# A fused cross-attention and expert layer: the first score visit, the expert tables and the last tiles are put in another order

## The chip, the core and the metric

The kernel runs on one core of a Trainium2 chip. The core has five engines that run side by side and wait for each other through semaphores: TensorE (PE in the rows; PEld is its weight load), VectorE (DVE), ScalarE (ACT), GpSimd (POOL) and SyncE (SP), which here issues most of the DMA transfers. Each engine works through its own list of instructions in the order in which they are written. The metric is the device time of one execution in microseconds (us).

## What is computed

For 16 batches of 256 tokens with 256 features, an attention layer over a context, then a layer of which one half is shared and the other half is one of two experts per token:

```python
x = x + xattn(layernorm(x), ctx, ctx, Wq, Wk, Wv, Wo)
x = x + ffn(layernorm(x), gate_w, w1, b1, w2, b2, sw1, sb1, sw2, sb2)
# xattn: 16 heads of 16; each block of 64 keys has a softmax of its own; sum over the blocks of a band
# ffn, n tokens, D = 256, hidden 1024:
top1 = argmax(softmax(x @ gate_w.T))
masked = x[None] * one_hot(top1).T[:, :, None]            # zero rows for the expert not chosen
h = relu(einsum("end,edh->enh", masked, w1) + b1)
routed = (einsum("enh,ehd->end", h, w2) + b2).sum(0)
shared = relu(x @ sw1 + sb1) @ sw2 + sb2
return routed + shared
```

## The kernel before

One iteration does one batch (i) of attention, the shared half of the batch before (n = i - 1) and one tile of 256 routed tokens (m = i - 2). The tokens are queued in DRAM by expert; a tile is 256 rows of one expert's queue. Iterations 0 to 3 are written out (iteration 0 has no shared half, 0 to 2 have no tile), 4 to 14 are a hardware loop, 15 is written out, and behind it come the rest of tile 14, the shared half of batch 15, tile 15 and two left tiles (`FIRST_LEFT`, `SECOND_LEFT`), one for each expert's remainder.

All operands of products are split in a high half (ScalarE) and a low half (VectorE or GpSimd), and products are three matmuls.

- **Scores.** `visit(i, v)` (v = 0 to 3) makes four banks of scores (L528), two in `work`, two in `nd`; VectorE takes the negative maximum of each bank (`maximum`, L1081). A bank can be written again when its maximum is taken. `maxima` (L541) transposes all of them, and ScalarE, VectorE and two DMAs (`shift`) write them as extra rows of `QP`. `scores_t` (L551) makes the transposed scores, ScalarE the exponentials, `values` (L567) the products, VectorE a reciprocal and a product for each of eight pairs (`divide`, L1088 and L1090). Q and K come back from DRAM in two halves (`spread`); visit 0 uses half 0.
- **The end of an iteration.** `attention_out` (L581), `project_out` (L595), residual (`x`, L1096), norm, with the reciprocal deviation from GpSimd (L1312, L1315), `norm2_apply` (`xhat`, L1054), `prep_tokens` (L483), the halves of `Xs` (L1034), then the shared half's first up. `norm1_apply` is the same form on `xin`, for the batch after the next.
- **Units.** A hidden layer of 1024 is four units. `up` (L477, 12 matmuls) makes a unit in `hid`, ScalarE its two halves (`relu`, L884), GpSimd the low half (`hl`, L1321), `down` (L639, 12 matmuls) adds it to `acc`. A tile's first down is preceded by two matmuls of a `level` row.
- **Tables.** What the expert not chosen gives for a zero row is a constant: `table(e)` (L691, 24 matmuls) for each expert, from `table_relu` (ScalarE) and `table_low` (GpSimd), through `level_sum` and `level_low` (L1169). Before, table 0 runs in iteration 1 in front of `attention_out`, table 1 behind the first visit of iteration 2, and `shared_down(1, 0)` waits for both level rows.
- **Tiles.** `ranks` and `place` (GpSimd, L1344 to L1378) find each token's row in its queue; `queue_x` and `queue_y` scatter the tokens; SP waits for them, then loads W1 of the tile's expert and the tile's tokens `xt` (L324); `tile_tokens` (L483, from `xt`) transposes them. Behind iteration 15, `left` gives the rows of the remainders, SP writes padding rows behind both queues (`xq<-T`, `yq<-T`), loads the first expert's W1 again, and then the two left tiles.

## Time and profile before

| | before |
|---|---|
| median of three runs | 997.09 us (995.03 to 997.75) |
| the profiled execution | 994.35 us, span 992.2 us, mean granted TensorE clock 0.932 |
| TensorE busy | 830.1 us, 84% of the span |
| VectorE, ScalarE, GpSimd busy | 64%, 45%, 44% |
| loop iteration, from one `attention_out` to the next | 52.4 to 53.9 us |
| from the first up of tile 14 to the last matmul | 80.6 us |

The span goes from the first to the last instruction that the profiler recorded; the execution is 2 us longer. A time in front of a row is its start, from the span's start. In brackets stands how long the engine had been idle before the row and what it waited for. A granted clock of 1.00 is TensorE's full clock.

### The profile page before, as it was taken

Reading aid. Unit: us, or ns where it says so; the run is one execution under the profiler, and the core shown is the slowest. Engines: PE = TensorE matmul, PEld = TensorE weight load, DVE = VectorE, ACT = ScalarE, POOL = GpSimd, SP = SyncE. Lnnn points to the kernel's source line nnn. Section 1 sums busy time; section 2 is a strip of 40 time slices with the busy share of each in tenths; the row PEclk is TensorE's granted clock in tenths of the full one; section 3 lists DMA queues with packets and bytes.
Section 4 is the critical chain, followed back from the end, with each engine's and each line's share of the span. In section 5 each row is a group of like instructions: output and inputs, shape, how many; then the busy total and the mean of one; then the engine's idle time right before and its main releaser. Section 6 shows DMA issues by size and latency. Waiting matters only on the chain.

```text
span 992.2 us, 22821 instructions
## 1 busy us (share of the span) xinstructions
PE 830.1 (84%) x7862; PEld 682.5 (69%) x7862; DVE 631.1 (64%) x1126; ACT 446.9 (45%) x980; POOL 440.8 (44%) x816
## 2 busy tenths in 40 slices
PE   3277868789898989899998989898989899887874
PEld 2246647477786868686868777786868686757874
DVE  3665585666868586867677776868586867663000
ACT  2353342436354545445454636354545445453432
POOL 3653322324344453626353534444453635253734
PEclk9586888979999999999999999999999999998988
DMA  8666230343535262525343443535262534222720
GB/s 258 164 161 223 75 97 6 107 154 115 163 94 195 74 205 81 159 86 157 101 154 127 133 153 116 170 91 195 74 198 88 159 100 136 96 69 100 245 65 22
DMA packets 97386, 128.17 MB, mean 129 GB/s; under 512 B 14655, under 2 KB 82623, under 8 KB 97088
## 3 DMA queue, kind: packets, MB, share of 16 engines
q1 hardware_dynamic: 89760, 107.89, 35.1%
q0 software_dynamic: 6624, 18.95, 5.7%
q10 hardware_dynamic: 960, 0.79, 0.5%
q8 instruction: 25, 0.41, 0.2%
q14 instruction: 17, 0.14, 0.0%
HBM read 90.80 MB, written 37.04 MB: 129 GB/s over the span
## 4 chain that ended last, share of the span: by engine, by line
issue 33%; POOL 24%; PE 20%; DVE 10%; DMA 7%; ACT 2%; POOLq 1%; SPq 1%; ACTq 1%; DVEq 0%
POOL hl L1321 11%; PE hid L477 5%; PE acc L639 4%; PE nd L567 4%; DVE T L1088 4%; DVE nmax L1081 3%; POOL out L1401 2%; POOL xq L1384 2%; PE work L551 2%; DMA QP<-scratch_m 2%; POOL c_lo_t L1306 1%; POOL rstd L1315 1%; POOL idle L1302 1%; DMA scratch_m<-mT 1%; POOL yq L1391 1%
## 5 line engine op out<-in xcount | busy, mean ns | idle before, releaser
L1321 POOL TENSOR_TENSOR hl<-h,hh 128x256 fp32r<-128x256 f32 x264 | 192.2, 735 | 361.5 <-ACT hh L884 359.8
L1088 DVE RECIPROCAL T<-nd 128x256 f32<-128x256 f32 x128 | 224.3, 1753 | 87.1 <-PE nd L567 78.5
L874 ACT ACTIVATE PT<-work 128x512 f32<-128x512 f32 x256 | 140.2, 606 | 90.6 <-PE work L551 90.6
L884 ACT ACTIVATE h<-hid,bias 128x256 f32<-128x256 f32 x144 | 68.5, 476 | 157.1 <-PE hid L477 155.6
L477 PE MATMUL hid<-Xs,W 128*128 128x256 f32 x816 | 122.6, 305 | 8.7 <-DVE Xs L1034 8.7
L477 PEld LDWEIGHTS hid<-Xs,W 128*128 128x128 f32 x816 | 110.8, 207 | 15.3 <-issue 9.1
L639 PE MATMUL acc<-w_hi,hh 128*128 128x256 f32 (+1 forms) x528 | 113.3, 297 | 3.5 <-DVE level L1169 3.5
L477 PE MATMUL hid<-Xr,W 128*128 128x256 f32 x768 | 105.1, 286 | 2.1 <-DVE Xr L1034 2.1
L639 PE MATMUL acc<-w_lo,hh 128*128 128x256 f32 (+1 forms) x528 | 106.2, 283 | 0.0
L477 PEld LDWEIGHTS hid<-Xr,W 128*128 128x128 f32 x768 | 94.8, 189 | 14.9 <-issue 10.7
L1081 DVE TENSOR_REDUCE nmax<-work 128x8 f32<-128x512 f32 x128 | 82.2, 685 | 33.4 <-PE work L528 33.1
L567 PE MATMUL nd<-PT,V 128*32 128x256 f32 x1024 | 84.5, 402 | 12.5 <-DVE T L1090 9.4
L639 PEld LDWEIGHTS acc<-w_hi,hh 128*128 128x128 f32 x528 | 82.3, 193 | 16.4 <-issue 10.6
L884 ACT ACTIVATE h<-hid,bsel 128x256 f32<-128x256 f32 x120 | 57.7, 481 | 71.4 <-PE hid L477 68.4
L639 PE MATMUL acc<-w_hi,hl 128*128 128x256 f32 (+1 forms) x528 | 85.3, 284 | 1.5 <-POOL hl L1321 1.5
L639 PEld LDWEIGHTS acc<-w_lo,hh 128*128 128x128 f32 x528 | 82.6, 193 | 0.0
L1081 DVE TENSOR_REDUCE nmax<-nd 128x8 f32<-128x512 f32 x128 | 82.0, 683 | 0.0
L567 PE MATMUL nd<-PT,bsum 128*32 128x256 f32 x1024 | 81.1, 388 | 0.0
L551 PE MATMUL work<-QP,KP 56*128 56x256 f32 x512 | 66.2, 337 | 16.6 <-DMA QP<-scratch_m 14.2
L551 PEld LDWEIGHTS work<-QP,KP 56*128 56x128 f32 x512 | 39.6, 190 | 50.5 <-ACT PT L874 22.0
L639 PEld LDWEIGHTS acc<-w_hi,hl 128*128 128x128 f32 x528 | 72.5, 193 | 2.6 <-POOL hl L1321 2.6
L884 ACT ACTIVATE hh<-hid,bias 128x256 fp32r<-128x256 f32 x144 | 68.5, 476 | 0.0
(178 smaller groups left out, 1384.0 us busy)
## 6 DMA issues: line engine op xcount, KB each, us to landing
W<-w1q SPq DMA_DIRECT2D x64, 512.0 KB, 6.1
KP<-scratch_k SPq DMA_DIRECT2D x192, 64.0 KB, 2.3
QP<-scratch_q SPq DMA_DIRECT2D x180, 64.0 KB, 2.3
scratch_k<-T SPq DMA_DIRECT2D x16, 512.0 KB, 3.5
scratch_q<-T SPq DMA_DIRECT2D x16, 512.0 KB, 3.3
yt<-yq SPq DMA_DIRECT2D x17, 260.0 KB, 2.9
xt<-xq SPq DMA_DIRECT2D x17, 256.0 KB, 3.7
xin<-x SPq DMA_DIRECT2D x16, 256.0 KB, 3.5
```

The lines of the kernel that those rows point to most:

```text
L477: mm = nc.tensor.matmul(dst, R(s), R(m), start=n == 0, stop=n == len(steps) - 1)
L551: mm = nc.tensor.matmul(banks[s][:, SEQ * t:SEQ * t + SEQ], R(KP[rows, p, P * t:P * t + P]), R(QP[rows, p, :]), start=True, stop=True)
L567: mm = nc.tensor.matmul(nd[r:r + 32, p % 2, kind, :], V[:, t, 2 * p + s, :] if kind == 0 else bsum[:, :], PT[:, (2 * p + s) % 4, t, :], st ...
L639: mm = nc.tensor.matmul(acc[:, t, :], R(h[:, u % 2, a, P * t:P * t + P]), R(row), start=first, stop=u == UNITS - 1 and h is hl and a == 1, ...
L874: nc.scalar.activation(PT[:, j % 4].rearrange("p t q -> p (t q)"), work[:, BANK[("st", j)], :], ACT.Exp).then_inc(sem["exp_done"], 1)
L884: last = nc.scalar.activation(dst, hid[:, u % 2, a, :], ACT.Relu, bias=bias[:, 2 * u + a:2 * u + a + 1])
L1081: nc.vector.tensor_reduce(nmax[:, t, :].rearrange("q (b s p) -> q s p b", s=2, b=NBLK) [:, s, 2 * g:2 * g + 2, :], bank.rearrange("q (n b ...
L1088: nc.vector.reciprocal(T[:, p, :], nd[:, p % 2, 1, :]).then_inc(sem["inverted"], 1)
L1302: nc.gpsimd.tensor_tensor(idle[:, site:site + 1], eps[0:1, 0:1], eps[0:1, 0:1], ALU.add)
L1321: nc.gpsimd.tensor_tensor(R(hl[:, u % 2, a]), h32[:, u % 2, a], hh[:, u % 2, a], ALU.subtract).then_inc(sem["hl_done"], 1)
L1384: pool.indirect_dma_start(out=xq, out_offset=bass.IndirectOffsetOnAxis(ap=pos[:, t:t + 1], axis=0), in_=xhat2[:, t, :], in_offset=None).th ...
L1401: pool.indirect_dma_start(out=out_rows, out_offset=bass.IndirectOffsetOnAxis(ap=rows, axis=0), in_=yt[:, t, 0:D], in_offset=None, **partly) \
```

## The change

TensorE's, VectorE's, ScalarE's and GpSimd's lists are reordered; no product is added or left out.

- `visit(i + 1, 0)` stands behind `attention_out(i)`; its four maxima stand two ahead of the residual and two ahead of `norm2_apply`. `norm1_apply` moves to VectorE's end of the iteration. The bank of `wo` changes, and with it what each bank waits for.
- An iteration begins with visit 1, then both ups, the ranks, the first down. In iterations 1 and 2 `shared_down` 1 stands ahead of visit 3, not behind it.
- Table 0 stays in iteration 1, table 1 goes to the same place in iteration 2; each level row is finished an iteration later, kept in `yt` in place of `xt`; the shared downs wait for `level_sum` of their own table only.
- In iteration 15 `tile_up` 1 stands ahead of the first `scores_t`, `tile_tokens` ahead of a down, `tile_down` 0 of the next tile ahead of `prep_tokens`; GpSimd takes the reciprocal deviation ahead of the low halves, and waits for the shift rows ahead of `place`.
- From unit 2 of tile 14 on, the low halves are VectorE's (`last_low`), `tile_tokens` stands ahead of the tile before's unit 3, and SP loads the first left tile's tokens ahead of its wait for `y_queued`. GpSimd leaves out its small operation `apart(7)` where the tile is not the loop's.

```diff
                 load_w1(W1[:, 0], 0, u, "w1_again")
+            sp.wait_ge(sem["padded"], 64)
+            rows = [sp.value_load(left[0:1, e:e + 1], min_val=0, max_val=QROWS - TILE) for e in range(2)]
+            sp.wait_ge(sem["xr_full"], FIRST_LEFT - 1)
+            load_tile_x(FIRST_LEFT, rows[0])
             sp.wait_ge(sem["y_queued"], 32 * BATCH)
             load_tile_y(last, row)
-            sp.wait_ge(sem["padded"], 64)
-            rows = [sp.value_load(left[0:1, e:e + 1], min_val=0, max_val=QROWS - TILE) for e in range(2)]
-            for m, row in zip((FIRST_LEFT, SECOND_LEFT), rows):
-                sp.wait_ge(sem["xr_full"], m - 1)
-                load_tile_x(m, row)
+            sp.wait_ge(sem["xr_full"], SECOND_LEFT - 1)
+            load_tile_x(SECOND_LEFT, rows[1])
...
                         pe.wait_ge(sem["r_done"], n - 2)
-                    elif n == 2:
-                        pe.wait_ge(sem["y_done"], 2)
-                    elif n == 1:
-                        pe.wait_ge(sem["level_made"], 2)
+                    elif n > 0:
+                        pe.wait_ge(sem["level_sum"], n)
...
                 n, m = i - 1, i - 2
-                visit(i, 0)
-                if type(i) is int and i == 2:
-                    table(1)
+                visit(i, 1, more)
                 if shared:
                     shared_up(n, 0)
+                    shared_up(n, 1)
                     ranks(n, claim(i, ("rk", 0), tile=tile))
-                    shared_up(n, 1)
-                visit(i, 1)
-                if shared:
                     shared_down(n, 0)
-                visit(i, 2)
+                visit(i, 2, more)
                 if shared:
                     shared_up(n, 2)
-                if tile:
                     shared_down(n, 1)
-                visit(i, 3)
+                visit(i, 3, more)
                 if tile:
                     shared_up(n, 3)
                     shared_down(n, 2)
-                elif shared:
-                    shared_down(n, 1)
                 maxima(i)
...
                 for p in range(PAIRS):
-                    fill(n, m, tile, p, expert)
+                    if more or p != 0:
+                        fill(n, m, tile, p, expert)
                     if p + 1 < PAIRS:
...
                     values(i, p)
                 if tile:
                     tile_up(m, 3)
-                if type(i) is int and i == 1:
-                    table(0)
+                elif shared:
+                    table(i - 1)
                 attention_out(i, more)
+                if more:
+                    visit(i + 1, 0)
+                else:
+                    tile_tokens(m + 1, work[:, BANK["v", 0], :])
                 if tile:
                     tile_down(m, 2, expert)
-                if not more:
-                    tile_tokens(m + 1, work[:, BANK["v", 0], :])
                 project_out(i, more)
...
             pe.wait_ge(*low_done(2 * STAGES - 1))
             pe.wait_ge(*low_done(len(pieces) - 1))
@@ -788,15 +808,13 @@
             iteration(3, True, True, True)
             with pe.Fori(4, BATCH - 1) as i:
                 iteration(i, True, True, True)
-            iteration(BATCH - 1, True, True, False)
+            expert = iteration(BATCH - 1, True, True, False)
 
             last = BATCH - 1
+            tile_up(last - 1, 2)
+            tile_down(last - 1, 1, expert)
             pe.wait_ge(sem["x2_lo"], BATCH)
             ranks(last, work[:, 2, :])
-            expert = pe.value_load(chosen[0:1, 1:2], min_val=0, max_val=1)
-            tile_down(last - 1, 0, expert)
-            tile_up(last - 1, 2)
-            tile_down(last - 1, 1, expert)
             tile_up(last - 1, 3)
             tile_down(last - 1, 2, expert)
             shared_up(last, 0)
...
                 tile_down(m, 0, expert)
                 tile_up(m, 2, weights, tokens)
                 tile_down(m, 1, expert)
-                tile_up(m, 3, weights, tokens)
                 if after:
                     tile_tokens(after[0], work[:, (after[0] - last) % 2, :])
+                tile_up(m, 3, weights, tokens)
                 tile_down(m, 2, expert)
...
 
+            def last_low(g, u):
+                for a in range(2):
+                    dve.wait_ge(sem["relu_done"], 2 * g + a + 1)
+                    nc.vector.tensor_tensor(R(hl[:, u % 2, a]), h32[:, u % 2, a], hh[:, u % 2, a],
+                                            ALU.subtract).then_inc(sem["last_low"], 1)
+
             def level_sum(e):
-                dve.wait_ge(sem["table_full"], 2)
-                nc.vector.tensor_tensor(xt[:, e, :], acc[:, e, :], bias2[:, :], ALU.add) \
+                dve.wait_ge(sem["table_full"], e + 1)
+                nc.vector.tensor_tensor(yt[:, e, 0:D], acc[:, e, :], bias2[:, :], ALU.add) \
                     .then_inc(sem["level_sum"], 1)
...
                 norm1 = more and (type(i) is not int or i + 2 < BATCH)
-                for v in range(VISITS):
+                for v in range(1, VISITS):
                     for j in range(4 * v, 4 * v + 4):
                         maximum(i, j)
                     splits(i, v + 1)
-                    if type(i) is int and i == 2 and v == 0:
-                        level_sum(0)
-                        level_sum(1)
-                    if shared and v == 0:
+                    if shared and v == 1:
                         rank_tokens(n)
-                    if type(i) is int and i == 2 and v == 0:
-                        level_low(0)
-                        level_low(1)
+                    if type(i) is int and i in (2, 3) and v == 1:
+                        level_low(i - 2)
...
                 low(i, "at_hi", work_bank("at"), a_hi[:, :, :], a_lo[:, :, :], "at_lo")
                 splits(i, 10)
-                if norm1:
-                    norm1_apply(i + 2)
-                if not more:
+                if more:
+                    maximum(i + 1, 0)
+                    maximum(i + 1, 1)
+                else:
                     tile_low(m + 1, work_bank("v"))
                 residual(i)
                 norm2_stats(i)
+                if more:
+                    maximum(i + 1, 2)
+                    maximum(i + 1, 3)
+                else:
+                    finish_tile(m)
                 norm2_apply(i)
...
-                if tile:
+                if tile and more:
                     finish_tile(m)
+                if shared and not tile:
+                    level_sum(n)
+                if norm1:
+                    norm1_apply(i + 2)
 
...
             nc.vector.memset(pad[:, :, D:YCOLS].bitcast(I32), SKIPPED).then_inc(sem["pad_made"], 1)
+            last_low(tile_unit(last - 1, 2), 2)
+            last_low(tile_unit(last - 1, 3), 3)
+            last_low(shared_unit(last, 0), 0)
             finish_tile(last - 1)
+            last_low(shared_unit(last, 1), 1)
+            last_low(shared_unit(last, 2), 2)
             tile_low(last, work[:, 0, :].rearrange("p (c t) -> p c t", c=2))
+            last_low(shared_unit(last, 3), 3)
+            last_low(tile_unit(last, 0), 0)
             finish_shared(last)
             for m, tokens in ((last, Xs), (FIRST_LEFT, Xr), (SECOND_LEFT, None)):
+                last_low(tile_unit(m, 1), 1)
+                last_low(tile_unit(m, 2), 2)
                 if tokens is not None:
                     tile_low(m + 1, work[:, (m + 1 - last) % 2, :].rearrange("p (c t) -> p c t", c=2), tokens)
+                last_low(tile_unit(m, 3), 3)
+                if tokens is not None:
+                    last_low(tile_unit(m + 1, 0), 0)
                 finish_tile(m)
...
                 if shared:
+                    if not more:
+                        pool.wait_ge(sem["shift_spread"], 32 * (i + 1))
                     place(n, choosing=type(i) is not int or i > 1)
                     queue_x(n)
...
                     tile_hidden(m, 3)
-                if type(i) is int and i == 1:
-                    table_low(0)
+                if shared and not tile:
+                    table_low(n)
                 if norm1:
                     reciprocal_deviation(i + 2, 0)
+                reciprocal_deviation(i, 1)
                 if not more:
                     tile_hidden(m + 1, 0)
-                reciprocal_deviation(i, 1)
 
...
 
             last = BATCH - 1
+            tile_hidden(last - 1, 1)
             send_out(last - 2)
-            tile_hidden(last - 1, 1)
-            tile_hidden(last - 1, 2)
             place(last, at=2)
-            tile_hidden(last - 1, 3)
             queue_x(last)
-            shared_hidden(last, 0)
             nc.gpsimd.tensor_copy(left[:, 0:1], next0[:, :])
             nc.gpsimd.tensor_copy(left[:, 1:2], next1[:, :])
             nc.gpsimd.tensor_scalar(left[:, 2:3], count[:, :], -1.0, float(BATCH * SEQ + QUEUE), ALU.mult, ALU.add)
             nc.gpsimd.tensor_copy(left[:, 3:4], count[:, :]).then_inc(sem["left_made"], 1)
-            shared_hidden(last, 1)
             send_out(last - 1)
-            shared_hidden(last, 2)
-            shared_hidden(last, 3)
-            tile_hidden(last, 0)
             queue_y(last)
-            for u in range(1, UNITS):
-                tile_hidden(last, u)
-            for m in (last, FIRST_LEFT):
-                tile_hidden(m + 1, 0)
+            for m in (last, FIRST_LEFT, SECOND_LEFT):
                 send_out(m)
```

ScalarE's list changes with these (its halves follow the units), and the claims of banks and the semaphores' names.

TensorE, behind the last division of iteration 3, before and after (L581, in the changed kernel L596, is `attention_out`; L639, now L657, are the first matmuls of `tile_down` 2):

```order
L581 MATMUL work<-T,hsum 32x2x64 x16
L639 ISA
L639 MATMUL acc<-w_hi,hh 128x256 x2
L639 REGISTER_ALU
L639 MATMUL acc<-w_lo,hh 128x256 x2
```

```order
L596 MATMUL work<-T,hsum 32x2x64 x16
L541 MATMUL work<-KP,QP 128x256 x4
L541 MATMUL nd<-KP,QP 128x256 x4
L657 ISA
L657 MATMUL acc<-w_hi,hh 128x256 x2
```

The score visit (`work` and `nd` from `KP`, `QP`) is put between them.

TensorE, from `prep_tokens` of iteration 3 into the loop's first iteration, before (the score visit, L528, is visit 0) and after (L541, it is visit 1; L488 is the up, L627 to L631 are the ranks):

```order
L483 MATMUL work<-id,xhat 128x128 x4
L789 UNCONDITIONAL_BRANCH
L469 REGISTER_ALU
L522 ISA
L528 MATMUL work<-KP,QP 128x256 x4
L520 REGISTER_ALU
L528 MATMUL nd<-KP,QP 128x256 x4
L621 ISA
L477 MATMUL hid<-Xs,W 128x256 x12
L612 MATMUL work<-mask,before 128x2
L614 MATMUL work<-mask,ones 128x2
L616 MATMUL work<-mask,ones 128x1
```

```order
L480 REGISTER_ALU
L535 ISA
L541 MATMUL work<-KP,QP 128x256 x4
L531 ISA
L541 MATMUL nd<-KP,QP 128x256 x4
L636 ISA
L488 MATMUL hid<-Xs,W 128x256 x12
L636 REGISTER_ALU
L488 MATMUL hid<-Xs,W 128x256 x12
L627 MATMUL work<-mask,before 128x2
L629 MATMUL work<-mask,ones 128x2
L631 MATMUL work<-mask,ones 128x1
```

The ranks stood between the two ups, and the next visit behind the second; now the two ups and the ranks follow each other, and the first down comes next.

SP behind iteration 15, from the second set of W1 loads, before and after:

```order
L320 DMA W<-w1q 128x1024 x4
L330 ISA
L330 DMA yt<-yq 128x2x260
L443 TENSOR_LOAD left
L443 ISA x2
L443 TENSOR_LOAD left
L443 ISA x2
L324 ISA
L324 DMA xt<-xq 128x2x256
```

```order
L328 DMA W<-w1q 128x1024 x4
L451 TENSOR_LOAD left
L451 ISA x2
L451 TENSOR_LOAD left
L451 ISA x2
L332 ISA
L332 DMA xt<-xq 128x2x256
L338 ISA
L338 DMA yt<-yq 128x2x260
```

The load of `xt` for the first left tile and the reading of `left` moved ahead of the load of `yt`.

## Rows read from the trace of the kernel before

**Rows 1.** TensorE's waits in iterations 4 to 14: total us, times, longest
```profile
PE work L483 <- DVE xhat L1054: 11.5, 11, 1.1
```
**Rows 2.** TensorE in order of time, iteration 6: start, us, line, tile, what it waited for
```profile
374.82 0.50 PE L528 MATMUL work<-KP,QP 48*128 48x256 f32 x4
...
375.97 0.50 PE L639 MATMUL acc<-w_hi,hh 128*128 128x256 f32 x2
...
377.57 0.50 PE L528 MATMUL work<-KP,QP 48*128 48x256 f32 x4
...
378.55 1.68 PE L477 MATMUL hid<-Xs,W 128*128 128x256 f32 x12
...
381.52 0.50 PE L528 MATMUL work<-KP,QP 48*128 48x256 f32 x4
...
382.19 1.68 PE L477 MATMUL hid<-Xs,W 128*128 128x256 f32 x12
```
**Rows 3.** TensorE in iteration 7, and the granted clock over its 4 us
```profile
424.03 2.93 PE L477 MATMUL hid<-Xs,W 128*128 128x256 f32 x12 [0.58 <-DVE Xs L1034]
...
424.00:428.00 4.00, 3.97 (x23) 3.88 (x24) 3.96 (x13) 0.87 (x3) 0.00 (x0) 0.62 0.30 117
```
**Rows 4.** VectorE at iteration 6's end, in order of time
```profile
418.09 0.69 DVE L1096 TENSOR_TENSOR x<-work,x 128x512 f32<-128x512 f32 x1 [1.00 <-PE work L595]
...
421.01 0.73 DVE L1054 TENSOR_SCALAR xhat<-x,mv,rstd 128x256 f32<-128x256 f32 x2 [1.16 <-POOL rstd L1315]
```
**Rows 5.** SP in order of time, iteration 6: half 0 of Q
```profile
402.38 2.78 SPq L259 DMA_DIRECT2D QP<-scratch_q  x6
```
**Rows 6.** TensorE in iterations 1 and 2, in order of time
```profile
136.84 1.08 PE L581 MATMUL work<-T,hsum 128*32 128x128 f32 x32 [0.15 <-DVE T L1090]
...
144.25 1.09 PE L483 MATMUL work<-id,xhat 128*128 128x128 f32 x4 [2.44 <-DVE xhat L1054]
...
160.90 0.80 PE L639 MATMUL acc<-w_hi,hh 128*128 128x256 f32 x2 [3.47 <-DVE level L1169]
...
200.10 1.94 PE L581 MATMUL work<-T,hsum 128*32 128x128 f32 x32 [3.27 <-DVE T L1090]
...
209.61 0.63 PE L483 MATMUL work<-id,xhat 128*128 128x128 f32 x4 [1.31 <-DVE xhat L1054]
```
**Rows 7.** TensorE in iteration 15, in order of time
```profile
869.55 0.50 PE L551 MATMUL work<-QP,KP 56*128 56x256 f32 x4 [2.73 <-DMA QP<-scratch_m]
```
**Rows 8.** Behind iteration 15: busy times, TensorE's waits, two ups of one pair apart
```profile
898.40:979.10 80.70, 65.27 (x510) 62.89 (x508) 10.04 (x32) 33.47 (x84) 46.53 (x81) 0.92 0.34 109
...
PE work L483 <- DMA xt<-xq: 5.7, 1, 5.7
PE work L483 <- DVE xhat L1054: 3.0, 1, 3.0
...
PE hid L477 <- DVE Xr L1034: 2.1, 2, 1.1
...
958.43 1.58 PE L477 MATMUL hid<-Xs,W 128*128 128x256 f32 x12
...
961.28 1.56 PE L477 MATMUL hid<-Xs,W 128*128 128x256 f32 x12
```
**Rows 9.** Behind iteration 15: GpSimd's `place`, SP's loads; issues with us to landing
```profile
915.60 0.20 POOL L1344 TENSOR_TENSOR own<-ids,rank 128x2 f32<-128x2 f32 x1
...
925.43 0.37 SPq L324 DMA_DIRECT2D xt<-xq  x1
...
933.29 0.37 SPq L435 DMA_DIRECT2D yq<-T  x1
...
946.39 0.39 SPq L324 DMA_DIRECT2D xt<-xq  x1
...
yq<-T SPq DMA_DIRECT2D x2, 260.0 KB, 7.0
xt<-xq SPq DMA_DIRECT2D x2, 256.0 KB, 2.7
```

106 lines of the change are left out of this document (63 added, 43 removed).

## The prediction, made before the changed kernel was run

> **What bounds the kernel now.** I read the page first (it has TensorE busy for 84% of the span), then TensorE's waits over eleven loop iterations, one iteration of TensorE and VectorE in order of time, then the places where an iteration is not like the others: iterations 1 and 2, iteration 15, and the stretch behind it. In the loop TensorE is nearly full. What it waits for in eleven iterations is 11.5 us for `xhat` (1.05 each) [rows 1], beside 1.5 us each for the divisions and less for other things. The outer stretches are poorer: in iteration 2 it waits 3.47 us for `level` and 3.27 us for `T` [rows 6], before the scores of iteration 15 it waits 2.73 us [rows 7], and behind iteration 15 it is busy for 65.27 of 80.70 us [rows 8]. A second loss is the clock: one first-layer unit takes 1.68 us at full clock [rows 2] and 2.93 us in iteration 7, where the granted clock over 4 us was 0.62, a stretch partly at 1.2 GHz, after TensorE had idled before `xhat` and `Xs` [rows 3]. By their starts, five of iterations 4 to 15 have such a slow first unit, at some 1.25 us each.
>
> **Part 1, the loop: the first visit moves to the end of the iteration before.** A visit whose banks are free takes 382.19 - 381.52 = 0.67 us. The second took 375.97 - 374.82 = 1.15, the third 378.55 - 377.57 = 0.98 [rows 2]: 0.48 and 0.31 us of waiting for VectorE, which at an iteration's start has sixteen maxima to take, as fast as it can. Now it has twelve there; the other four go into holes of the end: VectorE idles 1.00 us before the residual and 1.16 us before `xhat` [rows 4], and a pair of maxima takes 1.28 us there (a page row: 685 ns each). Added at the start is `norm1_apply`, 0.73 us by the same form in [rows 4], against 2.5 us that went. So both waits should go: 0.79 us, and some 0.6 us in an iteration with a slow first unit, which gives VectorE time. The visit itself costs 0.67 us at either place: it is ahead of `project_out` now, so `wo_full`, the residual and `xhat` come 0.67 us later, while visit 1 stands where visit 0 stood between `xhat`'s transposes and the first unit; the 1.05 us wait for `xhat` stays. The second pair of maxima fills the hole before `xhat` with 0.1 us to spare or less: I charge 0.05. New is that the first down follows the second up at once. Its low halves on GpSimd come about 2.6 us after the first up's end and are wanted about 2.6 us after it, so I charge 0.05 and keep 0.6 as the other end. Sum: 0.6 us for each of iterations 3 to 15, 13 x 0.6 = **7.8 us**; ends 0 and 10. Slow first units I leave as many as they are, since the idle time ahead of them keeps its shape; ends: none (-6) and one in every iteration (+9).
>
> **Part 2, the tables over two iterations.** Before, both tables and the level rows lie on iteration 2's path. `xhat`'s transposes of the last batch start at 144.25 and the first down at 160.90, 16.65 us [rows 6]. In the new order only these stand between: from transposes to first unit 2.55 us (the chain through ScalarE and VectorE in iteration 1's start, visit 1 beside it) and two ups partly at the low clock, 5.0 us; that is 7.55, so 9.1 us go. Iteration 1 itself I put 0.8 us earlier: its first residual no longer stands behind `norm1_apply`, which waited for GpSimd, and its visits lose their waits. From the first down to the transposed maxima nothing changes: before 8.6 us, now a down, a visit, an up and a down (5.4 us) and the 3.17 us from visit 3's begin to its last maximum, which no down covers any more. The new 1.07 us of `level` low halves on VectorE hide beside an up and a down. 9.1 + 0.8 = 9.9 us; 9.8 with 0.1 for a late maximum. The second table now runs in iteration 2 ahead of `attention_out`, where TensorE waits 3.27 us for `T`. In iteration 1 the first table ran in that place, and what was left of the wait was 0.15 us [rows 6]: it is free. It also keeps the clock: from `T` to `xhat` iteration 1 took 144.25 - 136.84 = 7.41 us and iteration 2, where `attention_out` ran 1.94 us instead of 1.08, took 9.51 [rows 6]; 2.1 us between them, of which I take 1.5 (the visit and the maxima may take 0.1, and the end may be slow for the reason of Part 1). Sum 9.8 + 1.5 = **11.3 us**; ends 9 and 13.
>
> **Part 3, iteration 15.** With `tile_up` 1 ahead of the first `scores_t`, it fills 1.6 of the 2.73 us that TensorE waits for the shift rows [rows 7], and the first values follow at once. Before, it ran behind that wait. VectorE's divisions start by that much earlier and set the rest of the iteration: **1.7 us**; ends 0 and 2.2.
>
> **Part 4, behind iteration 15.** From its first `tile_up` (898.47) to the last matmul 80.6 us pass. Work: 20 ups and 20 downs. A pair takes 961.28 - 958.43 = 2.85 us [rows 8], less with the level matmuls taken out, 2.83: 56.6 us; four level sets at 0.25, four transposes at 0.36 and the ends make 59.4. What the change does to the rest: the `xhat` wait of 3.0 us [rows 8] and the waits for the mask and for `yt` behind it go, since GpSimd takes the reciprocal deviation before the low halves and `tile_down` 0 stands in front of the transposes; the two waits for `Xr` (1 us each) go, as an up and a down now stand between transposes and use; the low halves of VectorE take away the waits for GpSimd, 1.5 us of the 15.4 that TensorE idles here (80.70 - 65.27) (nothing if they are late too). The largest wait, 5.7 us for `xt` [rows 8], does not go whole. Count from the first `tile_up` as zero. `ranks` stand at 7.7, `place` can start at 8.1 (before 17.1, [rows 9]), and since the load of `xt` came 925.43 - 915.60 = 9.8 us after that start with one pair of low halves between, now gone, it is issued at 16.6. Landing took 2.7 us [rows 9]: 19.3, wanted at 19.1, so 0.5 us is lost. The next load of `xt` waits for the padding: the last pad was issued 933.29 - 925.43 = 7.9 us after the first load and takes 7.0 us to land [rows 9], so 31.5; reading the two rows cost 1.35 us, and landing 2.7: **35.6**. TensorE is there at 31.9. It waits 3.7 us, not 5.7, but 15 us sooner (before, that load landed at 50.6), and restarts as slowly as before. From there 29.9 us are left as before (up 3 added, one `Xr` wait and 0.4 us of the last low halves off). End at 65.5 against 80.6: **15.0 us**; ends 12 and 19.5 (the load lands in time and the clock stays). The trace shows no load of `xt` issued while the second set of W1 loads is in flight; its nearest rows are 2.7 us on an empty queue and 7.0 us for a pad behind loads [rows 9]. I take 2.7, since by 33 most of that set has landed.
> On this the Trainium skill's page DMA: Bandwidth & Descriptors, "Issuing engines are not separate DMA queues", says that all DMAs run on the same 16 engines and interleave. The 7.0 us of a pad agrees, and by the rule alone the load would land some 1 us later and the sum be 1 us smaller. The page SBUF — State Buffer, "Who interferes with whom", says that a two-input operation of VectorE contends with GpSimd's reads; no row used here shows it in this stretch, and by it the 1.5 us of the low halves could come back in part.
> The final `send_out` loses one small operation of GpSimd: 0.3 us.
>
> **Sum.** 7.8 + 11.3 + 1.7 + 15.0 + 0.3 = 36.1 us. The profiled execution took 994.35 us (span 992.2), which gives 958.3; the median of the timed runs is 2.7 us above it, so 997.1 - 36.1 = **961.0 us**.
>
> **Rivals.**
> A, the load in time: pads and W1 loads land sooner and `xt` costs nothing, 4.5 us more gained: 956.5. For it: the wait is a difference of two long chains. Against: the pads' 7.0 us.
> B, the low clock in each iteration: seven more slow first units at 1.25 us: 961.0 + 8.8 = 969.8. For it: `xhat` is 0.05 us later and the idle time stays. Against: the added visit in front of it is work.
> C, the wait of `nmax` is replaced by one for GpSimd's low halves, since nothing stands between second up and first down: 0.6 us in 13 iterations: 968.8. For it: wanted and ready fall together. Against: GpSimd has nothing else to do there, its 0.73 us are short of a down's 1.5.
> D, the tables or iteration 15 give half or less, because the second table's low half is late and `T`'s hole doesn't hold it (5.5 us for 24 matmuls at the low clock against 3.27): 967 to 971.
> E, **slower than before**: VectorE takes two maxima ahead of the residual, so that a late visit holds up `wo`'s chain and with it all of the iteration's end. The visit needs the spread Q and K of the next batch, and each us that they come late is paid in each of 12 iterations. The kernel is slower from 36.1 / 12 = 3.0 us of lateness on; at 3.5 us it takes 1003. The last of half 0 is issued by 405.2 in one iteration [rows 5] and lands some 2.4 us later, the visit would come at 415: 7 us of room, so the spread would have to take 10 us longer than it does.
> F, the change doesn't do what it says: the waits go but every stage is held by VectorE at another place: within 0.3% of before. VectorE is busy 64% of the span; I see no such place.
>
> **Chances.** Forecast (957 to 965) 0.50, A 0.18, B 0.11, C 0.09, D 0.08, F 0.02, E 0.02. The range holds the forecast, A, C, B and most of D: 953 to 971. Faster by over 0.3% (3 us, about what a measurement can tell from no change) 0.96, within 0.3% 0.02, slower 0.02.
>
> **What the profile after would show.** Part 1: visits of 0.67 us everywhere in the loop, periods near 51.7 and 53.1 us instead of 52.4 and 53.7, no `nmax` wait; a wait of `acc` for `hl` would be C; a first unit of 2.9 us in each iteration B. Part 2: no table between `xhat` and the first unit, first down 7.5 us behind the transposes, no `T` wait in iteration 2. Part 3: two `scores_t` in a row, first values 1.7 us sooner. Part 4: one wait of some 4 us for `xt` some 32 us behind the first `tile_up`, none for `Xr` and `xhat`; 65 us in all. The prediction is wrong if TensorE shows a wait in each iteration that is not among these.

## The result

| | before | changed, first measurement | changed, second measurement |
|---|---|---|---|
| median of the runs | 996.06 us (4 runs, 992.78 to 997.75) | 954.64 us (4 runs, 952.14 to 957.01) | 953.58 us (6 runs, 948.65 to 956.68) |
| ratio to before | | 0.9588 (0.9546 to 0.9629) | 0.9574 (0.9539 to 0.9609) |
| profiled execution, span | 994.35, 992.2 us | 952.14, 950.3 us | 952.34, 950.5 us |

The second measurement's ratio is to its own runs of the kernel before (996.53 us, 11 runs). The kernel is 41.4 us faster in the first measurement (forecast 36.1, 961.0 us, range 953 to 971). By stretches of the two kernels' traces, the second trace of the changed kernel behind the slash:

| stretch | before | changed | gained | forecast |
|---|---|---|---|---|
| start to `attention_out` of iteration 3 | 255.3 | 241.0 / 239.3 | 14.3 / 16.1 | 11.9 |
| eleven periods, to that of iteration 14 | 583.3 | 571.6 / 571.7 | 11.7 / 11.6 | 6.6 |
| one period, to that of iteration 15 | 54.1 | 52.7 / 52.6 | 1.5 / 1.6 | 2.3 |
| from there to the last matmul | 86.3 | 71.9 / 73.8 | 14.4 / 12.5 | 15.0 |
| behind the last matmul | 13.2 | 13.2 / 13.2 | 0.0 | 0.3 |

The forecast column is the prediction's parts put into these stretches: Part 2 and one 0.6, eleven times 0.6, Part 3 and one 0.6, Part 4, the end. "Period" is the time from one `attention_out` to the next.

### The profile page after: what moved, and what is told of

Its sections match the earlier page's. It is cut to its first block, busy times and chain, and to the rows that moved or that the text cites. A ratio compares the mean times of both kernels' runs of the same rounds, so it can differ in the third digit from the quotient of the medians.

```text
span 950.3 us, 22814 instructions
## 1 busy us (share of the span) xinstructions
PE 812.9 (86%) x7862; PEld 673.6 (71%) x7862; DVE 645.9 (68%) x1162; ACT 445.9 (47%) x980; POOL 416.1 (44%) x773
## 4 chain that ended last, share of the span: by engine, by line
PE 59%; DVE 17%; DMA 11%; ACT 4%; issue 3%; SPq 2%; POOL 1%; ACTq 1%; POOLq 0%; DVEq 0%
PE hid L488 17%; PE acc L657 14%; PE nd L582 11%; DVE T L1104 7%; PE work L566 5%; DMA QP<-scratch_m 5%; DMA scratch_m<-mT 3%; DVE nmax L1097 3%; PE work L610 3%; PE work L541 2%; PE work L596 2%; PE work L494 1%; DVE xhat L1070 1%; DVE T L1106 1%; ACT h L902 1%
## 5 line engine op out<-in xcount | busy, mean ns | idle before, releaser
L1364 POOL TENSOR_TENSOR hl<-h,hh 128x256 fp32r<-128x256 f32 x228 | 166.7, 737 | 309.5 <-ACT hh L902 309.1
L488 PE MATMUL hid<-Xs,W 128*128 128x256 f32 x816 | 118.3, 301 | 8.2 <-DVE Xs L1050 8.2
L488 PEld LDWEIGHTS hid<-Xs,W 128*128 128x128 f32 x816 | 108.5, 205 | 15.2 <-issue 8.8
L657 PE MATMUL acc<-w_hi,hh 128*128 128x256 f32 (+1 forms) x528 | 111.2, 292 | 0.0
L657 PE MATMUL acc<-w_lo,hh 128*128 128x256 f32 (+1 forms) x528 | 104.8, 280 | 0.0
L488 PE MATMUL hid<-Xr,W 128*128 128x256 f32 x768 | 104.1, 285 | 0.0
L488 PEld LDWEIGHTS hid<-Xr,W 128*128 128x128 f32 x768 | 94.0, 188 | 12.3 <-issue 10.7
L582 PE MATMUL nd<-PT,V 128*32 128x256 f32 x1024 | 84.5, 402 | 11.7 <-DVE T L1106 8.4
L657 PEld LDWEIGHTS acc<-w_hi,hh 128*128 128x128 f32 x528 | 80.7, 189 | 8.9 <-issue 7.2
L657 PE MATMUL acc<-w_hi,hl 128*128 128x256 f32 (+1 forms) x528 | 84.3, 282 | 0.1
L657 PEld LDWEIGHTS acc<-w_lo,hh 128*128 128x128 f32 x528 | 81.1, 190 | 0.0
L657 PEld LDWEIGHTS acc<-w_hi,hl 128*128 128x128 f32 x528 | 71.6, 189 | 0.8 <-POOL hl L1364 0.3
```

Of the source, the lines that this page charges most:

```text
L488: mm = nc.tensor.matmul(dst, R(s), R(m), start=n == 0, stop=n == len(steps) - 1)
L582: mm = nc.tensor.matmul(nd[r:r + 32, p % 2, kind, :], V[:, t, 2 * p + s, :] if kind == 0 else bsum[:, :], PT[:, (2 * p + s) % 4, t, :], st ...
L657: mm = nc.tensor.matmul(acc[:, t, :], R(h[:, u % 2, a, P * t:P * t + P]), R(row), start=first, stop=u == UNITS - 1 and h is hl and a == 1, ...
L1364: nc.gpsimd.tensor_tensor(R(hl[:, u % 2, a]), h32[:, u % 2, a], hh[:, u % 2, a], ALU.subtract).then_inc(sem["hl_done"], 1)
```

## The profile after

**The loop.** TensorE in order of time in iterations 6 and 7 (start, us, line, operation, tiles, shape, number of instructions, and in brackets the idle time ahead and what ended it). L596 is `attention_out`, L541 a visit, L488 an up, L494 the transposes:

```profile
344.22 1.08 PE L596 MATMUL work<-T,hsum 128*32 128x128 f32 x32 [1.53 <-DVE T L1106]
345.23 0.51 PE L541 MATMUL work<-KP,QP 48*128 48x256 f32 x4
...
345.90 0.50 PE L657 MATMUL acc<-w_hi,hh 128*128 x2
...
354.96 3.09 PE L488 MATMUL hid<-Xs,W 128*128 128x256 f32 x24 [0.56 <-DVE Xs L1050]
...
359.72 0.50 PE L541 MATMUL work<-KP,QP 48*128 48x256 f32 x4
...
360.38 1.68 PE L488 MATMUL hid<-Xs,W 128*128 128x256 f32 x12
...
395.72 1.08 PE L596 MATMUL work<-T,hsum 128*32 128x128 f32 x32 [1.53 <-DVE T L1106]
```

Every visit now takes 0.67 us (345.90 - 345.23, 360.38 - 359.72 = 0.66), where [rows 2] has 1.15 and 0.98. Both first ups follow each other (3.09 for 24 matmuls), and a period is 51.50 us where nothing disturbs it. The waits for `xhat` and `Xs` stay as they were in [rows 1] and [rows 3]. TensorE's waits from the `attention_out` of iteration 3 to that of iteration 15 have no `nmax` and no `hl`; the two longest (total us, times, longest) are these:

```profile
PE work L596 <- DVE T L1106: 18.5, 12, 1.6
PE work L494 <- DVE xhat L1070: 12.5, 12, 1.1
```

**VectorE** at the same place of iteration 7, which answers to [rows 4]. The first pair of maxima ends 1.13 us ahead of the residual, the second ends as `xhat` can start, and the `xhat1` step (L1070 again, at 407.83) stands last:

```profile
398.11 1.28 DVE L1097 TENSOR_REDUCE nmax<-work 128x8 f32<-128x512 f32 x2
400.52 0.69 DVE L1112 TENSOR_TENSOR x<-work,x 128x512 f32<-128x512 f32 x1 [1.12 <-PE work L610]
...
402.19 1.26 DVE L1097 TENSOR_REDUCE nmax<-nd 128x8 f32<-128x512 f32 x2
403.44 0.73 DVE L1070 TENSOR_SCALAR xhat<-x,mv,rstd 128x256 f32<-128x256 f32 x2
```

**The clock.** Two of the eleven periods are longer, 53.00 and 54.36 us. The second is of a kind that the kernel before does not show. Stretches of TensorE behind the `attention_out` at 655.11 (window, its length, busy time of TensorE, of its weight loads, of VectorE, ScalarE and GpSimd, granted clock, DMA share, GB/s):

```profile
657.00:659.00 2.00, 2.00 (x10) 2.00 (x11) 1.77 (x3) 0.00 (x0) 0.08 (x1) 0.50 0.71 247
...
667.00:671.00 4.00, 3.59 (x18) 3.60 (x19) 3.96 (x13) 0.51 (x3) 0.00 (x0) 0.57 0.00 0
```

TensorE had idled 1.53 us before `attention_out`. Behind that and the visit the clock is at 0.50, which is 1.2 GHz, the third down takes 2.92 us, and the first ups at 667.4 are slow again: 2.8 us for the iteration. Below, a period with one or both of these is called disturbed.

Iteration 15 is not free of it in either trace of the changed kernel. In the first the clock falls behind the wait for the shift rows, in the second in the first ups:

```profile
846.00:848.00 2.00, 2.00 (x22) 0.94 (x20) 1.41 (x1) 0.79 (x2) 1.73 (x9) 0.51 0.03 8
```
```profile
822.00:824.00 2.00, 2.00 (x12) 2.00 (x11) 2.00 (x7) 0.00 (x0) 0.00 (x0) 0.53 0.06 19
```

In the traces of experiments 7 and 10, which leave iteration 15 as it is, it stays at full clock, and the period takes 51.23 and 50.97 us, not 52.66 and 52.55.

**Iterations 1 and 2**, TensorE, answering to [rows 6]. L709 is a table; some rows between are left out:

```profile
133.13 1.08 PE L596 MATMUL work<-T,hsum 128*32 128x128 f32 x32
...
141.21 0.91 PE L494 MATMUL work<-id,xhat 128*128 128x128 f32 x4 [2.45 <-DVE xhat L1070]
...
148.66 0.48 PE L657 MATMUL acc<-w_hi,hh 128*128 128x256 f32 x2
...
183.78 0.58 PE L709 MATMUL acc<-w_hi,hh 128*128 128x256 f32 x1
...
187.65 1.08 PE L596 MATMUL work<-T,hsum 128*32 128x128 f32 x32
...
195.73 0.82 PE L494 MATMUL work<-id,xhat 128*128 128x128 f32 x4 [2.46 <-DVE xhat L1070]
```

From the transposes to the first down 7.45 us pass (forecast 7.5, before 16.65), the second table fills the hole before `T`, and from `T` to `xhat` it is 8.08 us (forecast 9.51 - 1.5 = 8.0).

**Behind iteration 15**, which answers to [rows 8] and [rows 9]. TensorE's waits (the first up of tile 14 starts at 871.04), GpSimd's `place` and the last queued row, and SyncE's issues:

```profile
893.41 0.66 PE L494 MATMUL work<-id,xt 128*128 128x128 f32 x4 [2.52 <-DMA xt<-xq]
...
899.03 0.62 PE L657 MATMUL acc<-w_hi,hl 128*128 128x256 f32 x4
...
902.09 0.50 PE L697 MATMUL acc<-level,level_row 128*128 x2 [1.03 <-DVE yp L1163]
...
908.48 0.66 PE L494 MATMUL work<-id,xt 128*128 128x128 f32 x4 [1.64 <-DMA xt<-xq]
```
```profile
879.77 0.19 POOL L1387 TENSOR_TENSOR own<-ids,rank 128x2 f32<-128x2 f32 x1 [0.38 <-DVE count L1149]
...
882.66 0.50 POOL L1410 TENSOR_SCALAR chosen<-ahead,which,next 128x1 int32<-128x1 f32 x1
...
886.08 0.97 POOL L1427 DMA_INDIRECT xq<-xhat,pos  x1 [0.30 <-issue]
```
```profile
885.62 0.34 SPq L328 DMA_DIRECT2D W<-w1q  x1
890.01 0.37 SPq L332 DMA_DIRECT2D xt<-xq  x1
890.56 1.39 SPq L328 DMA_DIRECT2D W<-w1q  x3
892.15 0.33 SPq L359 DMA_DIRECT2D bsel<-b  x1
...
897.04 2.02 SPq L328 DMA_DIRECT2D W<-w1q  x4
903.88 0.39 SPq L332 DMA_DIRECT2D xt<-xq  x1
```

The last matmul ends at 937.13: 66.1 us, 68.1 in the second trace (forecast 65.5, before 80.6). The same columns as above over the whole stretch, first and second trace, for which [rows 8] has 80.70 us, 65.27 busy and 0.92:

```profile
871.04:937.14 66.10, 60.77 (x509) 59.41 (x507) 25.25 (x66) 33.69 (x84) 21.54 (x41) 1.00 0.40 132
```
```profile
869.20:937.31 68.11, 62.25 (x509) 61.02 (x507) 25.92 (x66) 33.62 (x84) 21.43 (x41) 0.97 0.40 129
```

So TensorE idles 5.3 and 5.9 us and not 15.4; the other 4.4 and 3.0 us are the same matmuls in less busy time, at a mean clock of 1.00 and 0.97 and not 0.92. There are two waits for `xt`, at +19.9 and +35.8 us, and a new one of 1.03 us for `yp`. Why `yp` is late stands in ScalarE's and VectorE's rows:

```profile
899.24 0.47 ACT L902 ACTIVATE h<-hid,bsel 128x256 f32<-128x256 f32 x1 [2.15 <-DMA bsel<-b]
```
```profile
900.85 0.43 DVE L1180 TENSOR_TENSOR hl<-h,hh 128x256 fp32r<-128x256 f32 x1 [0.31 <-ACT hh L902]
901.19 0.68 DVE L1162 TENSOR_TENSOR yp<-acc,x 128x512 f32<-128x512 f32 x1
```

`bsel`, the bias of the chosen expert, is issued behind four loads of W1 and lands 7.1 us later, the relu of the last tile's first unit waits 2.15 us for it, VectorE's low halves wait for the relu, and `yp` is queued behind them, though the shared expert's last matmuls had ended by 899.03 + 0.62 = 899.65.

## Experiments

All start from the changed kernel. Times are medians of five or six runs.

**1. The changed kernel once more.**

> The changed kernel once more, for a second trace of it beside the others. If the number of iterations in which TensorE's clock is low at the end or in the first unit is a matter of chance (2 of 12 in its first trace, and 2, 2 and 7 in the three kernels that keep its loop), it may be anything from 0 to 7 here, every undisturbed period is 51.5 to 51.7 us again, and the time is 952 to 960, moving with that number by 1.4 to 2.9 us each. If the number belongs to the kernel, it is 2 and the time 952 to 956.

953.58 us. The undisturbed period is 51.45 to 51.72 again; two of eleven periods are disturbed, one of each kind (52.8 and 54.4). The number came out the same, but with the traces below it is no property of the kernel: it was 2 to 6 in the kernels that keep its loop.

**2. The visit back to the iteration's start.** Its four maxima go back there with it, and `norm1_apply` stands ahead of the residual again.

```diff
-                visit(i, 1, more)
+                visit(i, 0)
                 if shared:
                     shared_up(n, 0)
-                    shared_up(n, 1)
                     ranks(n, claim(i, ("rk", 0), tile=tile))
+                    shared_up(n, 1)
+                visit(i, 1)
...
-                    visit(i + 1, 0)
```

> The changed kernel with Part 1 alone undone: visit 0 stands at the iteration's start again, with its four maxima there and the xhat1 step in front of the residual; the first two shared ups have ranks and visit 1 between them. Theory (Part 1 as forecast): the visits' waits of some 0.48 and 0.31 us come back in each iteration, the undisturbed period goes from 51.55 back to 52.4 us, and 12 to 13 iterations give 8 to 11 us; with about as many slow first units as in the changed kernel (2 of 12) 963 to 966 us. Rival 1: the visit's place also decides how often TensorE's clock falls ahead of the first unit: then 4 or more of the 12 iterations show a first unit of 2.9 us, and the time is 967 to 970. Rival 2: the loop's gain comes from elsewhere, the period stays under 51.9 and the time under 958.

973.17 us (971.03 to 975.24), beyond both expectations. An undisturbed period, L591 being `attention_out`, is 455.58 - 403.23 = 52.35 us, and the waits for `nmax` are back:

```profile
403.23 1.08 PE L591 MATMUL work<-T,hsum 128*32 128x128 f32 x32 [1.54 <-DVE T L1100]
...
455.58 1.08 PE L591 MATMUL work<-T,hsum 128*32 128x128 f32 x32 [1.54 <-DVE T L1100]
```
```profile
PE nd L538 <- DVE nmax L1091: 3.2, 11, 0.3
```

The span is 969.5, 19.1 more than the mean of the changed kernel's two: 3.5 to iteration 3 (1.8 in the period from iteration 0 to 1, 2.2 in the next), 12.2 in eleven periods, 2.3 in iteration 15 and 1.1 behind it. Of the 12.2, 11 x 0.87 = 9.6 are the undisturbed period (52.47 us in the mean against 51.60), and 2.6 that six periods are disturbed and not two. Iteration 15 and the stretch behind it also have more low clock here. So the visit is worth some 13 us beside the clock, the first two iterations being the uncertain part (see Part 1 below). Of the waits' list only 0.3 us an iteration is named `nmax`; the period shows the rest, so this list alone would have undersized the part.

**3. The tables back in iteration 2**, with both level rows ahead of its first shared down.

```diff
                 visit(i, 1, more)
+                if type(i) is int and i == 2:
+                    table(1)
...
-                elif shared:
-                    table(i - 1)
+                elif i == 1:
+                    table(0)
                 attention_out(i, more)
```

> The changed kernel with Part 2 alone undone: both tables are made for iteration 2's first shared down, the second one at that iteration's start. Theory (Part 2 as forecast): from the transposes of xhat to iteration 2's first down it takes some 16 us and not 7.45, TensorE waits for T again by 3.3 us in iteration 2 and from T to xhat takes 9.5 us and not 8.1: 11 us slower than the changed kernel (9 to 13), 964 to 968. Rival: of the 14.3 us by which the changed kernel is ahead at iteration 3, 3 and more came from earlier stretches and the visit; then the tables give back 8 us or less, 960 to 962.5.

965.22 us. TensorE waits for `level` ahead of the first down and for `T`:

```profile
140.59 0.63 PE L494 MATMUL work<-id,xhat 128*128 128x128 f32 x4 [2.45 <-DVE xhat L1080]
...
156.25 0.79 PE L657 MATMUL acc<-w_hi,hh 128*128 128x256 f32 x2 [4.12 <-DVE level L1201]
...
195.40 1.93 PE L596 MATMUL work<-T,hsum 128*32 128x128 f32 x32 [3.27 <-DVE T L1116]
```

That is 15.66 us from transposes to first down against 7.45, and from `T` to `xhat` 10.17 against 8.08. At iteration 3's `attention_out` (249.6) it is 9.5 us behind the mean of the changed kernel's two traces. The median says 10.6 to 11.6; the loop is the changed kernel's, but this trace had six disturbed periods (15.7 us), so the trace's stretch is the better measure: 9.5. That is below the expected 11 and in its range of 9 to 13.

**4. Iteration 15's second `tile_up` back behind the scores.**

```diff
                     tile_up(m, 0)
-                    if not more:
-                        tile_up(m, 1)
```

> The changed kernel with Part 3 alone undone: in iteration 15 the second tile_up stands behind the first scores_t again. Theory (Part 3): TensorE waits some 2.7 us and not 1.5 for the shift rows, attention_out of iteration 15 comes 1.2 to 1.7 us later, and the time is 956 to 956.5. Rival: VectorE's divisions make up for it by attention_out; nothing changes, 954.6 within 0.3.

960.52 us (957.28 to 967.02); the median does not settle 2 us, since the runs are 10 us apart. The trace says more. From the transposed maxima to `attention_out` it takes 870.87 - 838.79 = 32.08 us, and 865.28 - 835.15 = 30.13 in the changed kernel. The wait for the shift rows is 2.98 us and 1.52, and behind the longer one the displaced `tile_up` itself runs 2.93 us:

```profile
838.79 0.27 PE L556 MATMUL work<-id,nmax 128*128 128x128 f32 x1
...
846.48 0.79 PE L566 MATMUL work<-QP,KP 56*128 56x256 f32 x4 [2.98 <-DMA QP<-scratch_m]
847.20 2.93 PE L488 MATMUL hid<-Xr,W 128*128 128x256 f32 x12
...
870.87 1.08 PE L596 MATMUL work<-T,hsum 128*32 128x128 f32 x32 [1.61 <-DVE T L1101]
```

The 1.95 us between the two are not all the order's, for the clock is low in both places. From the first `scores_t` behind the wait to the third `tile_up` it takes 12.28 us here and 10.41 in the changed kernel's first trace; in its second, at full clock, it takes 8.86, and a `tile_up` more 1.6. So 1.8 of the 32.08 us and 1.5 of the 30.13 are the clock's, and without them it is 30.3 against 28.6 us (the second trace has 28.49). Part 3 is worth some 1.7 us (forecast 1.7).

**5. GpSimd makes the last low halves.**

```diff
+            tile_hidden(last - 1, 2)
             place(last, at=2)
+            tile_hidden(last - 1, 3)
             queue_x(last)
+            shared_hidden(last, 0)
...
-            last_low(tile_unit(last - 1, 2), 2)
-            last_low(tile_unit(last - 1, 3), 3)
```

> The changed kernel with GpSimd making all the low halves behind iteration 15 again, in the places that it had before. Theory: two pairs of 1.45 us come back ahead of the queueing of the last tokens, so that the waits for xt grow by 2 to 3 us; with the waits of downs for low halves of 1.5 us it is 4 to 5 us slower, 958.5 to 959.5. Rival 1: only the direct waits come back, 956. Rival 2: VectorE's low halves cost as much (they make the level matmuls wait 1.03 us for yp): 954 to 955.

956.00 us (952.66 to 965.58), again too wide for the question. From tile 14's first up to the last matmul it takes 71.2 us, 4.1 more than the mean of 66.1 and 68.1. TensorE's idle time is only 0.9 us of that (6.5 against 5.3 and 5.9). Another 2 us are the clock: behind the 3.19 us wait shown below, the transposes, an up and a down take 6.03 us against 3.27 and 4.87. The rest is open. Four waits for `hl` come first, of 2.06 us together, of which the first is the longest; the wait for `xt` behind them is hidden, and the next one is 3.19:

```profile
884.59 0.50 PE L654 MATMUL acc<-w_hi,hl 128*128 x2 [1.08 <-POOL hl L1358]
...
910.22 1.12 PE L491 MATMUL work<-id,xt 128*128 128x128 f32 x4 [3.19 <-DMA xt<-xq]
```

SyncE issues the first `xt` at +19.6 us here and at +19.0 in the changed kernel: two pairs of low halves (2.9 us) gone from ahead of it gave 0.6. The rows show two things that took the rest. GpSimd's own steps are slower while VectorE makes low halves: `chosen` takes 0.34 us here,

```profile
882.35 0.34 POOL L1404 TENSOR_SCALAR chosen<-ahead,which,next 128x1 int32<-128x1 f32 x1
```

and 0.50 above; `place` from `own` to its last step takes 4.05 us here and 4.56 there. The Trainium skill's page SBUF — State Buffer, "Who interferes with whom", says that a two-input operation of VectorE and GpSimd's reads get in each other's way, and this agrees, at 0.5 us. And the last queued row, 2.73 us from its issue to the load of `xt` here, takes 3.93 there, where 512 KB of W1 were issued 0.46 us ahead of it and not 1.8. That the W1 load is the cause is argued from these two rows and not tested by itself; other traces with the load as close have 3.54 to 4.06 us.

**6. SyncE's order of before.**

```diff
-            load_tile_x(FIRST_LEFT, rows[0])
             sp.wait_ge(sem["y_queued"], 32 * BATCH)
             load_tile_y(last, row)
+            load_tile_x(FIRST_LEFT, rows[0])
```

> The changed kernel with one thing undone: SyncE loads the y rows of the last tile, for which the last tokens' yq must be queued, ahead of the xt of the first leftover tile, as before the change. Theory: queueing yq ends about 37 us behind the first tile_up (GpSimd issues it at 31.6 to 33.8, once yp is made), so that xt is issued at 38 or later and not at 32.8 and TensorE waits for it some 5 us longer, 6.6 and not 1.6: 71 us for the stretch, 959 to 960. Rival: the y rows are queued earlier than that and the load is as late anyway, since it waits for the pads: 954.6 within 1.

962.18 us. The stretch takes 72.4 us, 5.3 more than the mean. TensorE idles 3.2 us more (8.8 us); the other 2.1 us are a mean clock of 0.93 and not 1.00 and 0.97. The load of `xt` stands behind that of `yt` at 913.38, which waited for `yq`, and TensorE waits 6.50 us:

```profile
913.38 0.39 SPq L338 DMA_DIRECT2D yt<-yq  x1
915.13 4.45 SPq L332 DMA_DIRECT2D xt<-xq  x2
```
```profile
917.91 1.12 PE L493 MATMUL work<-id,xt 128*128 128x128 f32 x4 [6.50 <-DMA xt<-xq]
```

**7. `norm1_apply` ahead of the residual again.**

```diff
+                if norm1:
+                    norm1_apply(i + 2)
                 if more:
                     maximum(i + 1, 0)
...
-                if norm1:
-                    norm1_apply(i + 2)
```

> The changed kernel, but the xhat1 step of the batch after next stands in front of VectorE's residual again, as before the change, now with the first pair of maxima behind it. Theory: in the loop VectorE idles 0.89 and 1.12 us ahead of the residual beside the pair of maxima, so that 0.73 us more still fit, the period stays at 51.6 within 0.1; only in iterations 1 and 2, where GpSimd makes the table's low half first, the residual comes later, by up to 1 us each: 955 to 957 with the same clock. Rival: the hole is full; residual and xhat come 0.3 us or more later in each iteration, the wait for xhat is 1.4 us and not 1.05: 4 us and more, 959 and above.

956.76 us, with one run at 967. In the trace the undisturbed period is 51.6 as before and the wait for `xhat` 12.6 us in twelve: the hole ahead of the residual takes 0.73 us more, as its 1.12 us say. In iteration 0 `xhat` comes 2.3 us later behind `attention_out`, made up for by iteration 3. So the step's new place is worth nothing in the loop.

**8. The transposes of tokens behind the fourth up**, in the last shared half and the tiles behind it.

```diff
+                tile_up(m, 3, weights, tokens)
                 if after:
                     tile_tokens(after[0], ...)
-                tile_up(m, 3, weights, tokens)
```

> The changed kernel, but behind iteration 15 the transposes of the next tile's tokens stand behind the fourth up again (shared_up 3 or tile_up 3), as before the change. Theory: that up fills 1.6 us of each wait for xt, 2.5 to 1.0 and 1.6 to 0.1, and the waits for Xr or Xs that come back are under 0.5 us each: the stretch takes 64 us and not 66.1, time 952 to 953. Rival: the three waits for Xr and Xs are 1 us each again and nothing is gained: 954.6.

955.29 us; the stretch takes 66.0 us, as the better of the two traces of the changed kernel. The waits for `xt` are 0.43 and 1.99, but `Xr` costs 0.38 and 1.02 again: the order moves waits between `xt` and `Xr`, as the rival said.

**9. Another order of the last loads, and `yp` first.** GpSimd queues the last tokens before it chooses a tile. The pads now follow unit 1; `load_tile` had issued W1's unit 0, `xt`, units 1 to 3 and `bsel`.

```diff
-            last_low(tile_unit(last, 0), 0)
             finish_shared(last)
+            last_low(tile_unit(last, 0), 0)
...
+                if at:
+                    queue_x(n)
                 apart(2)
...
-            row = load_tile(last, at=2)
+            sp.dma_start(bsel[:, :], b1[:, bass.ds(HT * expert + HT, HT)]).then_inc(sem["bias_loaded"], 16)
...
+            load_tile_x(last, row)
+            load_w1(W1[:, 1], expert, 0)
+            load_w1(W1[:, 1], expert, 1)
...
+            load_w1(W1[:, 1], expert, 2)
+            load_w1(W1[:, 1], expert, 3)
...
+            load_tile_x(FIRST_LEFT, rows[0])
             for u in range(UNITS):
...
                 load_w1(W1[:, 0], 0, u, "w1_again")
-            load_tile_x(FIRST_LEFT, rows[0])
```

> The changed kernel with another order of the loads and of two steps behind iteration 15: GpSimd queues the last tokens as soon as their places are known, ahead of choosing the next tile; SyncE issues bsel, then xt, W1 units 0 and 1, the four pads, units 2 and 3, and the xt of the first leftover tile ahead of the second set of W1; VectorE makes yp ahead of the low halves of the last tile's first unit. Theory: xt is issued 16 us behind the first tile_up and not 19.0, and lands in time (2.5 us gone); the pads no longer stand behind 2 MB of W1, so that the first leftover xt is there in time (1.6 us); the wait of 1.03 us for yp goes. The stretch takes 61 us and not 66.1, the time is 949 to 951. Rival 1: the transfers only swap places, and TensorE waits for W1's units 2 and 3 instead: 952 to 954. Rival 2: only the yp wait goes: 953.6.

949.30 us (948.77 to 955.61), ratio to before 0.9544 (0.9511 to 0.9578); the stretch takes 62.65 us. The waits for `yp` and for the second `xt` are gone; the first `xt`, issued at 889.55 (+17.8), costs 1.72, and W1's unit 2 0.30. The clock stays full in the stretch. The three changes were not run apart; each is read from its own wait:

```profile
893.31 0.66 PE L504 MATMUL work<-id,xt 128*128 128x128 f32 x4 [1.72 <-DMA xt<-xq]
```

**10. The same, with the choice reported at once and `xt` issued first.** W1's units 2 and 3 each follow a pair of pads.

```diff
+                if at:
+                    wait(9)
+                    nc.gpsimd.tensor_tensor(idle[:, 0:1], eps[0:1, 0:1], eps[0:1, 0:1], ALU.add).then_inc(sem["placed"], 1)
                 nc.gpsimd.tensor_scalar(taken[:, :], which[:, :], float(TILE), None, ALU.mult) \
...
+            load_tile_x(last, row)
             expert = sp.value_load(chosen[0:1, 3:4], min_val=0, max_val=1)
```

> The kernel new_end, further: GpSimd reports the last tile's choice as soon as it is made, ahead of moving the counters; SyncE issues xt ahead of bsel and reading the expert, and W1's unit 2 between the two pairs of pads. Theory: in new_end xt was issued at 889.55, 2.0 us behind that report and 1.7 us too late; now it is issued by 888.2 and TensorE waits 0.4 us at most for it, and not at all for W1: the stretch from the first tile_up to the last matmul takes 61 us and not 62.7, the time is 947 to 948. Rival: the queued tokens land no earlier than 889, so that xt can't be issued before: nothing gained, 949.3.

948.79 us (945.29 to 950.39), ratio 0.9517 (0.9484 to 0.9550). `xt` is issued 889.09 - 873.55 = 15.5 us behind the first up and costs nothing. Now the second `xt`, issued at 903.52 behind the pads, costs 1.36, so that 61.8 us are left of 66.1:

```profile
906.42 0.66 PE L503 MATMUL work<-id,xt 128*128 128x128 f32 x4 [1.36 <-DMA xt<-xq]
```

This is the lowest median of all, 5 to 6 us below the changed kernel's, but the runs don't tell it from experiment 9's. The expected 61 us was missed by the second `xt`.

**11. The visit behind the third down.**

```diff
-                visit(i + 1, 0)
                 tile_down(m, 2, expert)
+                visit(i + 1, 0)
```

> The changed kernel, but at an iteration's end the next batch's first visit stands behind the third tile_down and not between attention_out and it. The eight traces with the visit in its new place show, in 12 of 88 loop iterations, a tile_down of 2.9 us and not 1.65 behind that visit, at a clock of 0.50, and a slow first unit behind it too (2.8 us in all); the two with the visit at the iteration's start show none in 22. Theory: the visit's short products behind attention_out's short ones are what lets the clock fall there; with the down between them none of 11 iterations shows it, the undisturbed period stays 51.6, and the runs spread less: 952 to 954, none over 957. Rival 1: the clock falls after the idle time before attention_out whatever stands behind it: 1 or 2 of 11, time and spread as for the changed kernel. Rival 2: the maxima now come 1.6 us later, and with them the residual and xhat: the period is 52 and more, 959 and above.

956.05 us (954.06 to 959.92), and with experiment 10's end, whose expectation follows, 950.85 (946.05 to 953.05).

> new_end2 and visit_second together. Theory of both: 945 to 947, no iteration with a slow tile_down. If visit_second is slower, this is slower than new_end2 by the same amount.

In 22 periods of these two traces, six have slow first ups and none a slow down. The two kernels with the visit at the iteration's start had eleven in 22, also without a slow down. With the visit right behind `attention_out`, ten traces have 31 disturbed periods in 110, and 17 of them show the slow down as well. So the slow down goes with the visit right behind `attention_out`. At a frequency of 17 in 110, 22 periods without one happen by chance 2 or 3 times in 100, and the 44 of both other places once in 1000 or less; this takes the periods as independent, which five slow downs in experiment 3's trace make doubtful. The cost does not go with it: what the disturbed periods take above the undisturbed ones is 12.8 us in 22 periods with the visit at the start, 67.5 in 110 with it behind `attention_out`, 0.58 and 0.61 us a period. With the visit behind the down it is 0.36, but the undisturbed period is 51.80, since `xhat`'s transposes come 0.2 us later. Neither kernel got faster, and the runs above 957 that I excluded came all the same.

## Why the prediction was right, and where it was off

The time is in the range, but below the 957 to 965 us of the forecast itself and nearest to rival A's 956.5, whose mechanism did not happen. What makes it 5 us faster than forecast is above all Part 1's size. Some 2 us more are luck: of the loop's 11.7 us, so much comes from five disturbed periods (6.1 us) in the trace before and two (4.2 us) in this one.

**Part 1** (7.8 us forecast, some 13 measured) had the right mechanism and too small a size. Both visits' waits went; a visit takes 0.67 us now. In an undisturbed iteration the change gives 52.47 - 51.60 = 0.87 us, where the 0.79 of [rows 2] were cut to 0.6. Two of the cuts were unneeded: no `xhat` delay (1.05 as before) and no wait for low halves. The third was right: a slow first unit alone costs 1.42 us above the undisturbed period now (14 periods) and 1.17 with the visit at the start (11), so that such an iteration gains 0.62. The rest of the miss is iterations 1 and 2, for which I had 0.8 us and experiment 2 shows 1.8 and 2.2. These two are not the visit's alone. In iteration 2 the last values stand 49.83 us behind `attention_out` in experiment 2 and 48.99 in the changed kernel, a difference of 0.8 us; the other 1.3 us come from there to the next `attention_out`, in the second table, where the granted clock was 0.54 in experiment 2 and 0.69 in the changed kernel. Iteration 1's period is 55.4 to 58.0 us in nine traces with the changed order, so that its 1.8 us are not clear of chance.

**The clock**, left as it was with a range of -6 to +9, was right by luck, for a reason that I did not have. The changed kernel disturbs fewer iterations (31 of 110, against 11 of 22) at a higher price. Rival B (a slow first unit in each iteration) did not happen. The profiled executions of the changed kernel had 4.2 and 4.0 us of it, where 11 x 0.61 = 6.7 are the mean, and lie 1 to 2.5 us under their medians.

**Part 2** (11.3, with 0.8 of the visit's in it) measured 9.5. The step from transposes to first down came out as worked out, 7.45 against 7.55, the second table was free in `T`'s hole, and `T` to `xhat` gave 1.43 of 1.5. The 0.8 belongs to Part 1. From the first down to the transposed maxima it took 8.43 us (forecast 5.4 + 3.17), with the wait for the last maxima, 2.43 us, that the 3.17 held; the low halves of `level` did not show as waits. Some 1.6 us of the start's gain lie ahead of iteration 0's `attention_out`, where the kernels have the same work; in the changed kernel and its variants it starts between 75.6 and 77.8, so that can be chance. Rival D (half) did not happen.

**Part 3** (1.7) came out as forecast, some 1.7 by its undoing. Between the kernels iteration 15 gained only 1.5 and 1.6 us, where this and the visit's 0.87 should give 2.6. The clock took the rest: it cost 1.3 to 1.7 us in iteration 15 of both traces of the changed kernel, as the two at full clock (51.23 and 50.97) show, and 0.6 in that of the kernel before, whose `tile_up` behind the shift rows took 2.26 us and not 1.6.

**Part 4** (15.0) measured 14.4 and 12.5, with errors that partly cancel. The term "issued at 16.6" failed: it was 19.0 and 18.5, for `place` came 0.4 to 0.6 us later, and taking a pair of low halves away (1.4 us) did not shorten the chain: from the start of `place` to the issue it took 10.2 and 10.0 us, and 9.9 with the pair in it, in experiment 5. So `xt` cost 2.5 and 1.9 us and not 0.5. The issue of the next `xt` at 32.9 was hit (32.8, 32.9). Its landing took 4.6 and 4.9 us and not 2.7, nearer the 7.0 of a pad than I took it; TensorE, late by the earlier waits, waited 1.6 and 3.8 for it.

All of TensorE's idle time is near what the sum had, 5.3 and 5.9 us against 65.5 - 59.4 = 6.1. "Restarts as slowly as before" held in the second trace (30.3 us from there to the end, forecast 29.9) and not in the first, where the clock stayed full (28.7), which is why the two differ. The clock fell behind this wait in seven of the eight traces in which it was 2.65 us or more, and in none of the four in which it was 1.99 or less.

As to the landing, the Trainium skill's page DMA: Bandwidth & Descriptors, "Issuing engines are not separate DMA queues", by which the load shares its engines with the second set of W1 loads and which made the sum 1 us smaller, was nearer than my row on an empty queue.

The wait for `yp` was not foreseen at all: VectorE got a queue in which a late `bsel` holds up what was ready, 1.03 and 0.19 us. The waits for low halves went (2.1 us of them come back in experiment 5), and so did those for `xhat`, for the mask and for `Xr` (3.0, 2.4 and 2.1 us before), which no experiment undoes by itself. Experiment 5's time, 956.00 us, is its rival 1's: only the direct waits come back; the waits for `xt` do not grow.

Rival A (the load in time, whose 4.5 us should have been 0.5 + 3.7 = 4.2) took more edits: experiment 9 for the second load, experiment 10 for the first, and not both at once.

**The end**: one small operation less gave nothing, 13.2 us before and after; the last transfers behind it don't start sooner by it. Rivals C, E and F: no wait for `hl` in the loop, the visit finds the next batch's Q and K there (at 345.23 without a wait), and the waits that went came back nowhere in the loop.

## What to carry to other kernels

Where an engine must take a burst of work at a stage's start, moving a quarter of it into the same engine's holes at the end of the stage before cost nothing here, where a hole was about as long as the piece; the period shows the gain, a list of waits only part of it. Work moved to a less busy engine also moves into that engine's order: ask for each thing queued behind it what its inputs wait for. In a tail of dependent loads, count the queue of the issuing engine in the order of need, since taking work from the chain ahead gave 0.6 us of 2.9 here, while another order of the loads with `yp` first gave some 4 us (experiment 9). And set a stretch of one trace against that of another only with the granted clock of both beside it.

## What the runs showed that I had not expected

The same kernel's runs lie 4 to 13 us apart, which is of the size of the smaller parts, and most of it goes with the mean granted clock (0.951 at 952.66 us, 0.932 at 965.23 in two runs of experiment 5's kernel). For parts of 1 to 5 us only one stretch of two traces can be compared, and then with the granted clock of both. A stretch at a granted clock of 0.50 appeared behind 1.5 us of idle time and the short products of `attention_out` and the visit, and not where the third down stood first, in the 22 periods of experiment 11's traces and the 22 with the visit at the iteration's start. And GpSimd's steps on one or two columns took up to twice as long (`ahead`, 0.39 us against 0.18) while VectorE subtracted.
